# Storing the residual in the loop and adding the FFN part with an accumulating scatter, in a gated expert layer on one Trainium2 core

## The reference

```python
def _L0_xattn_ref(hidden_states, token_ids, Wg, Wu, Wd):
    ...
    for e in range(E):
        g = jax.nn.silu(jnp.einsum('bsd,fd->bsf', hidden_states, Wg[e]))
        u = jnp.einsum('bsd,fd->bsf', hidden_states, Wu[e])
        y = jnp.einsum('bsf,df->bsd', g * u, Wd[e])
        out = jnp.where((expert_ids == e)[..., None], y, out)
    return out
...
x = x + jnp.tanh(g_xattn[0]) * _L0_xattn_ref(_layernorm(x, axis=-1), itok_BxS_13_99985, ctx_2048, ctx_2048, ctx_2048)
x = x + jnp.tanh(g_ffn[0]) * _L0_ffn_ref(_layernorm(x, axis=-1), L0_ffn_weight)
```

## Time and profile before

| what | us |
|---|---|
| median of three runs (lowest, highest) | 201.29 (201.24, 203.76) |
| the profiled execution | 201.43 |
| its span in the trace | 199.7 |
| busy: TensorE matmuls | 144.3 |
| busy: VectorE | 156.3 |
| busy: ScalarE | 112.7 |
| busy: GpSimd | 81.8 |

### The profile page before, as it was taken

One profiled execution on the slowest core, in us unless ns is written; L12 is line 12 of the kernel. 1 busy time (PEld: TensorE's weight loads), 2 busy tenths in 40 slices (PEclk: granted clock), 3 DMA queues, 4 the chain that ended last, 5 costly groups with the idle time before them and its releaser, 6 DMA issues.

```text
span 199.7 us, 3062 instructions
## 1 busy us (share of the span) xinstructions
PE 144.3 (72%) x723; PEld 69.7 (35%) x727; DVE 156.3 (78%) x351; ACT 112.7 (56%) x166; POOL 81.8 (41%) x117
## 2 busy tenths in 40 slices
PE   0141939998999797999998999999851266566600
PEld 0110424443555343544444445555420223223200
DVE  2876697798758799899989787776686999998820
ACT  2366596887524854688868534233313987666510
POOL 7158787320312344332386673001110023566670
PEclk9999996999999999999999999999997579999985
DMA  0937998200000222111212210000000002132351
GB/s 6 365 113 198 355 408 264 85 2 0 0 3 0 54 56 53 26 39 43 54 26 53 56 26 0 3 0 2 0 5 0 0 0 105 57 153 113 149 208 59
DMA packets 15440, 15.68 MB, mean 79 GB/s; under 512 B 10816, under 2 KB 11328, under 8 KB 15424
## 3 DMA queue, kind: packets, MB, share of 16 engines
q1 hardware_dynamic: 12576, 7.09, 11.8%
q0 software_dynamic: 2560, 8.39, 11.6%
q10 hardware_dynamic: 288, 0.00, 0.1%
HBM read 8.92 MB, written 4.19 MB: 66 GB/s over the span
## 4 chain that ended last, share of the span: by engine, by line
PE 38%; DVE 33%; issue 11%; POOL 7%; ACT 6%; DMA 1%; DVEq 1%; POOLq 0%
PE four_ps L465 10%; PE four_ps L457 10%; PE four_ps L470 9%; DVE w_hi L1044 3%; DVE hT_hi L1052 3%; PE four_ps L498 3%; POOL x L341 3%; PE four_ps L569 2%; DVE bn L880 2%; DVE zT_lo L866 2%; DVE bn L832 2%; DVE x L1056 2%; ACT y L703 2%; DVE z L861 2%; DVE w_lo L824 2%
## 5 line engine op out<-in xcount | busy, mean ns | idle before, releaser
L364 POOL DMA_INDIRECT out<-x,token_of x16 | 19.3, 1208 | 25.4 <-DVE x L1056 22.9
L359 POOL TENSOR_TENSOR rstd<-var,minus_half 128x1 f32<-128x1 f32 x16 | 8.8, 552 | 49.3 <-DVE var L888 49.3
L633 ACT ACTIVATE zT_hi<-four_ps 128x512 f16<-128x512 f32 x19 | 11.3, 595 | 18.9 <-PE four_ps L498 18.9
L457 PE MATMUL four_ps<-w_hi,hT_hi 128*128 x76 | 21.3, 394 | 0.8 <-ACT w_hi L596 0.7
L624 ACT ACTIVATE sg<-four_ps,job_inv_a 128x512 f32<-128x512 f32 x19 | 12.9, 679 | 15.4 <-PE four_ps L470 12.4
L341 POOL DMA_INDIRECT x<-in_x,token_of x16 | 17.4, 1088 | 7.0 <-issue 4.2
L457 PE MATMUL four_ps<-w_hi,zT_hi 128*128 x76 | 19.5, 379 | 0.8 <-ACT zT_hi L633 0.8
L465 PE MATMUL four_ps<-w_lo,hT_hi 128*128 x76 | 19.9, 384 | 0.0
L615 ACT ACTIVATE w<-x,nmr,rstd 128x512 f32<-128x512 f32 x16 | 13.0, 810 | 11.9 <-DVE nmr L894 11.5
L470 PE MATMUL four_ps<-w_hi,zT_lo 128*128 x76 | 19.5, 379 | 0.0
L465 PE MATMUL four_ps<-w_lo,zT_hi 128*128 x76 | 19.5, 379 | 0.0
(11 more groups left out here) (148 smaller groups left out, 293.4 us busy)
## 6 DMA issues: line engine op xcount, KB each, us to landing
w<-in_ctx_t SPq DMA_DIRECT2D x4, 1024.0 KB, 9.4
wf<-in_wf_t SPq DMA_DIRECT2D x1, 512.0 KB, 15.4
x<-in_x,token_of POOLq DMA_INDIRECT x16, 5.9
out<-x,token_of POOLq DMA_INDIRECT x16, 2.9
hT_hi<-h_row SPq DMA_TRANSPOSE x9, 2.3
hT_lo<-h_row SPq DMA_TRANSPOSE x9, 2.3
ids_s<-in_ids SPq DMA_DIRECT2D x1, 8.0 KB, 2.9
g_s<-in_g_x ACTq DMA_DIRECT2D x1, 0.5 KB, 2.7
```

What stands on the lines that cost most here:

```text
L364: pool.indirect_dma_start(out, bass.IndirectOffsetOnAxis(ap=token_of[:, i:i + 1], axis=0), block_of(x1, i), None, bounds_check=T - 1).then ...
L457: pe.matmul(ps, lhs_hi(k), w_block(w_hi, expert, k), start=(k == 0), stop=False)
```

## The change

The output is written twice. In the loop, when a tile of `x1` is complete, GpSimd scatters it to the output (`store_x1`): one such scatter per job from job 5 on, behind `rstd_second`, and the last after the loop. In the tail, `finish` no longer adds: it writes tanh of the gate times `y8` over the tile's block of `x1`, as a `tensor_scalar` with one tensor input, and GpSimd scatters that with a DMA that adds to what stands in the output (`add_tile`, `compute_op=ALU.add`). Two waits keep the order: GpSimd waits for all sixteen first scatters ahead of the first adding one, and VectorE waits for the same ahead of its first `finish`, which overwrites `x1`.

```diff
-        stored = sem("stored")
+        stored, x1_stored = sem("stored"), sem("x1_stored")
...
-            def store_tile(i):
+            def store_x1(i):
+
+                pool.wait_ge(x1_done, i + E)
+                pool.indirect_dma_start(out, bass.IndirectOffsetOnAxis(ap=token_of[:, i:i + 1], axis=0),
+                                        block_of(x1, i), None, bounds_check=T - 1).then_inc(x1_stored, 16)
+
+            def add_tile(i):
                 pool.wait_ge(out_done, through(i))
                 pool.indirect_dma_start(out, bass.IndirectOffsetOnAxis(ap=token_of[:, i:i + 1], axis=0),
-                                        block_of(x1, i), None, bounds_check=T - 1).then_inc(stored, 16)
+                                        block_of(x1, i), None, bounds_check=T - 1, compute_op=ALU.add)\
+                    .then_inc(stored, 16)
...
                 if E <= j:
                     rstd_second(j - E)
+                if E < j:
+                    store_x1(j - E - 1)
                 if WF_ROUNDED <= j < WF_ROUNDED + K:
                     wf_rounded(j - WF_ROUNDED)
...
             for j in range(1, TILES + E):
                 job(j)
+            store_x1(TILES - 1)
+            pool.wait_ge(x1_stored, 16 * TILES)
             for i in range(TILES):
-                store_tile(i)
+                add_tile(i)
             pool.wait_ge(stored, 16 * TILES)
...
             def finish(g):
                 dve.wait_ge(y8_done, g + 1)
-                dve.scalar_tensor_tensor(out=rows_of(x1, g), in0=ring(y8, g, NB), scalar=tg[:, 1:2],
-                                         in1=rows_of(x1, g), op0=ALU.mult, op1=ALU.add).then_inc(out_done, 1)
+                if g == 0:
+                    dve.wait_ge(x1_stored, 16 * TILES)
+                dve.tensor_scalar(rows_of(x1, g), ring(y8, g, NB), tg[:, 1:2], None, ALU.mult).then_inc(out_done, 1)
```

## The result

The changed kernel takes 214.94 us (median of four runs, 214.47 to 215.01) against 201.94 for the kernel before beside it (four runs, 201.24 to 203.76): a ratio of 1.062 [1.055, 1.070], 13.0 us slower. That is above the predicted range. The profiled execution has a span of 213.2 us against 199.7, so 13.5 us are to be found in the traces. Two marks cut the span into three: the start of the last second rstd, where the loop ends (149.63 before), and the end of the last scatter's issue (193.91 + 0.98 = 194.89 before).

A forecast was written before the change was run, and what follows sets the result against it. The prediction took VectorE to bound the FFN tail and GpSimd's scatters and the DMAs the end. It summed 201.43 + 1.5 (loop) - 0.2 (tail to last issue) + 1.0 (landing) = 203.7 us, range 199.8 to 210.0.

The forecast's parts named there:

- Part 2: Tail, GpSimd: 14 adding scatters at 1.2 us plus 0.30 between, plus 3.3 of port waits; last ends at 194.7, against 194.89.
- Jobs 5 to 9 ... Nothing: Loop: the store makes GpSimd's first rstd 0.83 us later, within a slack of 1.22, so these jobs lose nothing.
- Part 4: Loop: each store adds a GpSimd instruction of about 1.2 us; +1.5 us in all, ends 0.9 and 3.2.
- Part 3: Landing of the last scatter: an add reads its destination first, so +1.0 us, ends 0 and 3.0.
- Part 1: Tail, VectorE: finish takes 0.75 us a pair, 0.48 a single tile; addition of tiles 10 and 11 ends 2.2 us earlier.
- Rival B: Tail: GpSimd's adding scatter alone paces it, from about 1.25 us on; at 1.47, 207.5 us in all; chance 0.25.
- a scatter waits at its start for a running two-input instruction of VectorE: Tail: such waits cost GpSimd 0.6 us in four of ten scatters; instructions starting later neither hold it nor wait.
- the hold of up to 0.75 us: Tail: by the skill's two-port rule each new finish meeting a scatter holds it so long; sum longer by 1 or 2 us.
- Rival D: Tail: the transfers themselves pace it, at 2.9 us for each adding one; near 217 us in all; chance 0.08.
- The low half comes 1.2 later, but its transposes are for a product two jobs on: Loop, jobs 5 to 9: the store delays GpSimd's low half of h by 1.2 us, counted as costing nothing.
- the ring: Loop, jobs 10 to 12: GpSimd and VectorE wait on each other; two turns grow by 1.2 us each, 2.4.
- listed signs: Profile after: store about 1.0 us, first-rstd wait 0.66 to about 1.9, second shift 0.16, z's transposes about 1.5 late, adds 1.2.

The follow-up runs named there:

- experiment 4: The changed kernel with plain instead of adding scatters in the tail, leaving the residual out of the output: 207.53 us, ratio 1.028.
- (2): The changed kernel without the stores in the loop and their waits, leaving the residual out of the output: 207.98 us, ratio 1.028.
- (3): The changed kernel with each loop store one instruction earlier on GpSimd, ahead of the second rstd: 209.43 us, ratio 1.035.
- (6): The changed kernel with VectorE's second shift reading one tensor input, rstd as per-partition scalar: 213.53 us, ratio 1.054.
- (8): The changed kernel with the loop stores ahead of the second rstd and the second shift in one-input form: 208.37 us, ratio 1.031.
- experiment 5: The kernel before with only the last tile's scatter adding, onto output rows nothing has written: 204.12 us in one run.

## Why the prediction was wrong

The decisive step is Part 2's term for one adding scatter, and beside it "Jobs 5 to 9 ... Nothing" in Part 4 and the size of Part 3. No one of the three alone leaves the range: the largest, 4.4 us in the tail, would have made 203.7 into 208.1. Any two of them do.

**Part 1 was right.** The finish takes 0.75 and 0.48 us, and with plain scatters the tail gets 2.3 us shorter (experiment 4).

**Part 2, mis-sized.** "I take 1.2, near the plain one": it measured 1.54. The rest of the step holds: put 1.54 into its own formula and the last scatter ends at 170.4 + 14 x 1.84 + 3.3 = 199.5; measured, less the loop's 5.52, it is 199.04. 0.34 us fourteen times is 4.8, which turns the forecast's -0.2 into +4.6; the tail lost 4.2. The choice was made by nearness to the row of the plain scatter, and between the ends 0.98 and 1.96 the truth lay just past the middle. Rival B named the mechanism (GpSimd alone paces the tail from 1.25 us on) but took 1.47 as its price and the forecast's loop and landing with it. The Trainium skill's sentence quoted there (Collectives: The Full Stack, "The bandwidth ceiling: the fold count and why AG ≠ RS ≠ AR"), that an added transfer runs at half the rate of a copy, was on the right side; here it is 1.95 us against 0.72, less than half the rate.

That "a scatter waits at its start for a running two-input instruction of VectorE" is seen again: the add at 180.39 takes 2.49 us. VectorE's timeline beside it, in the kernel after:

```profile
180.25 1.23 DVE L1063 TENSOR_TENSOR hT_hi<-w_hi,hT_hi 128x1024 bf16<-128x1024 f32 x1
181.60 0.75 DVE L1069 TENSOR_SCALAR x<-y,tg 128x1024 f32<-128x1024 bf16 x1
```

The two-input instruction that runs as the scatter starts ends at 181.48, 1.09 us later, and the remaining 1.40 is nearly one adding scatter. The new finish, at 181.60 inside it, kept its 0.75 and held nothing up. That is not so of every scatter. The one at 187.54 takes 1.90 us, 0.36 more than one with nothing in the way, and no two-input instruction runs until 0.2 us before its end; the finish below ends 0.09 us ahead of it:

```profile
188.60 0.75 DVE L1069 TENSOR_SCALAR x<-y,tg 128x1024 f32<-128x1024 bf16 x1 [1.20 <-ACT y L714]
```

The same pair of rows stands in (2), (3), (6) and (8), with scatters of 1.90 or 1.91 us. So the hold of up to 0.75 us that the prediction named for a finish comes in part: no scatter here is held by the whole of one, and a finish of 512 columns inside the scatter at 191.91 left it at 1.55.

**Part 3, mis-sized.** "I take 1.0" is near what one add alone costs (1.1, experiment 5). Missing were 1.3 of queueing, since an adding transfer (1.95) is longer than the distance of their issues (1.85), and the 1.4 (5.0 less 3.6) by which the program ends later after 16 more GpSimd scatters of any kind: 3.8 in all. Rival D's idea, transfers that pace the end, was thus nearly true, at 1.95 us and not at 2.9.

**Part 4, half wrong.** For jobs 5 to 9 the prediction asked who waits for the first rstd, found a slack of 1.22 us, and that was right. The step that failed is "The low half comes 1.2 later, but its transposes are for a product two jobs on": it asked who waits for the low half, and not what the low half now runs beside. It runs beside VectorE's two-input shift and weight maximum and holds three of them, 3.65 us by job 8. The prediction knew the effect, having read it at 107.20, but used it only where the change takes it away. In the ring it was near: 1.33 and 1.34 for a turn where 1.2 was forecast. TensorE's transposes of z, 3.46 us late ahead of the ring (106.18 against 102.72), come another 1.10 and 1.71 later in it, where 0.3 and 1.6 were forecast. In the kernel after they stand here, and before at 109.14 and 115.25:

```profile
113.70 0.66 PE L509 MATMUL four_ps<-ident,z 128*128 128x128 f32 x4 [1.74 <-DVE z L872]
120.42 0.66 PE L509 MATMUL four_ps<-ident,z 128*128 128x128 f32 x4 [0.74 <-DVE z L872]
```

From job 10 to the last second rstd the loop loses 2.08 us (5.52 less 3.44), where 1.5 was taken for the ring. Of the listed signs, the store's 1.0 us, the shift's 0.16 in the ring's jobs, a wait of 2.20 us for the first rstd there (1.9 was named) and the covered waits came as said.

**What stays open.** Two of the three held instructions began while the store's scatter was still running (71.62 in one that ended at 71.80, 78.13 in one that ended at 78.87) and were held from then on, although a shift at 93.04, begun with a scatter, took 0.17. Whether the last part of a scatter holds VectorE too was not tried; in (4) the finish at 188.23, over the end of a scatter at 188.60, takes 0.89 us in place of 0.75. Nor was what makes the clock fall a second time in some tails.

## What to carry to other kernels

When an instruction is put on an engine off the critical path, look for the gap in which that engine idles, and ask of everything that it pushes not only who waits for it but what it will now run beside: one line of difference was 0.2 or 5.5 us here. Before a DMA takes over an addition, price it on its issuing engine (1.54 against 0.98 us), on the DMA engines (1.95 against 0.72 us) and in the landing of the last, and multiply by how many there are on the engine that ends last. Where a price is unknown and enters fourteen times, forecast from the middle of its bounds and not from the comfortable neighbour.

## What was not expected of the hardware

An adding indirect scatter of 128 rows makes 144 packets where a plain one makes 80, and takes 1.95 us of the DMA engines against a mean of 0.72. In kernels with sixteen more scatters from GpSimd, the end of the program is 1.3 us longer after the last data has moved (3.6 to 4.9); the cause is open. A VectorE instruction of a single column takes up to 1.41 us in place of 0.16 while GpSimd's elementwise instruction runs, and 0.21 in a form with one tensor input. And TensorE's clock falls to its lower level a second time in the tail of some executions, of the unchanged tail too, and two single executions can differ by more (2.5 us) than the loop was to gain.
